# Local-attention scores from 64-row products in two PSUM banks, and a ring of two banks in place of three

## The reference, cut to what matters

```python
for i in range(DEPTH):                                    # 6
    x = attn_layer(shift_tokens(x), Wqkv[i], q_scale[i], k_scale[i], Wo[i]) + x
    x = ffn_layer(shift_tokens(x), ln_g[i], ln_b[i], W1[i], b1[i], W2[i], b2[i]) + x

def attn_layer(...):          # 16 heads of 64, windows of 32 tokens
    q = l2norm(q) * qs ; k = l2norm(k) * ksc              # then rotary tables on both
    sim = einsum('bhwie,bhwje->bhwij', bq, bk2) * 8.0     # bk2: keys of the window and of the one before
    attn = softmax(where(mask, -max, sim), -1)
    out = einsum('bhwij,bhwje->bhwie', attn, bv2)
    return out @ Wo
```

## Time and profile before

| What | Value |
|---|---|
| time, median of 3 runs | 1903.41 us (1899.98 to 1903.65) |
| span of the profiled execution | 1897.4 us |
| runs shown, lowest and highest, less that span | 2.6 and 6.3 us |
| TensorE clock granted, mean | 0.985 |
| PE busy | 1775.2 us (94%) |
| DVE busy | 1620.6 us (85%) |
| POOL busy | 1278.1 us (67%) |
| ACT busy | 1157.9 us (61%) |
| DMA queue q1 | 43.5% of 16 engines |

### The profile page before, as it was taken

The page is one execution under the profiler, slowest core; times in us unless marked ns, Lnnn a source line. Parts: engine busy times, 40 slices in busy tenths (PEclk is TensorE's granted clock), DMA queues, the critical chain, the costliest instruction groups (busy, mean ns, idle before and its releaser), DMA issues.

```text
span 1897.4 us, 49036 instructions
## 1 busy us (share of the span) xinstructions
PE 1775.2 (94%) x19119; PEld 1213.9 (64%) x19119; DVE 1620.6 (85%) x2695; ACT 1157.9 (61%) x2003; POOL 1278.1 (67%) x1548
## 2 busy tenths in 40 slices
PE   7999998899999999999999999999999999999997
PEld 4545454466666666666666676666666766666675
DVE  5887785799889999899898989998999889989983
ACT  3565665456566656665666666655766666666665
POOL 5212124777688777787777788768877778777762
PEclk8999999899999999999999999999999999999999
DMA  2000011455545555555455555555555455555552
GB/s 77 1 6 1 7 41 45 155 176 172 176 161 186 181 170 165 178 174 183 163 173 172 170 179 172 187 166 169 181 183 173 164 173 183 170 180 166 188 164 80
DMA packets 190739, 275.62 MB, mean 145 GB/s; under 512 B 23278, under 2 KB 87340, under 8 KB 190252
## 3 DMA queue, kind: packets, MB, share of 16 engines
q1 hardware_dynamic: 189004, 270.48, 43.5%
q10 hardware_dynamic: 1504, 2.00, 0.3%
HBM read 72.11 MB, written 52.43 MB: 66 GB/s over the span
## 4 chain that ended last, share of the span: by engine, by line
PE 37%; DVE 29%; POOL 14%; issue 10%; ACT 8%; DMA 1%; ACTq 0%; POOLq 0%; DVEq 0%; SPq 0%
DVE turned L982 10%; DVE kz L1002 7%; PE psum L597 4%; PE psum L668 3%; PE psum L599 3%; PE psum L598 3%; PE psum L807 3%; PE psum L837 3%; DVE rd L1018 3%; PE psum L691 3%; PE psum L682 3%; POOL u L1425 3%; PE psum L741 2%; POOL sdiff L1414 2%; ACT hid L1291 2%
## 5 line engine op out<-in xcount | busy, mean ns | idle before, releaser
L982 DVE SCALAR_TENSOR_TENSOR turned<-psum,vecs,tabs 128x1024 f32<-128x1024 f32 x384 | 486.8, 1268 | 33.2 <-POOL u L1425 20.9
L1190 ACT ACTIVATE sq<-psum 128x512 f32<-128x512 f32 x384 | 227.8, 593 | 164.8 <-PE psum L599 164.0
L1414 POOL TENSOR_TENSOR sdiff<-sdiff,rqs 128x512 f32<-128x512 f32 x192 | 200.8, 1046 | 151.9 <-DVE sdiff L1014 151.6
L1425 POOL TENSOR_TENSOR qT<-turned,swapped 128x512 f32<-128x512 f32 x192 | 242.4, 1283 | 37.9 <-PE psum L775 36.6
L1425 POOL TENSOR_TENSOR u<-turned,swapped 128x512 f32<-128x512 f32 x192 | 241.5, 1279 | 37.2 <-DMA swapped<-turned 36.8
L1002 DVE TENSOR_TENSOR kz<-u,psum 64x512 f32<-64x512 f32 x384 | 255.3, 665 | 6.3 <-PE psum L763 3.7
L796 PEld LDWEIGHTS psum<-pxT,v 128*64 128x64 f32 x6144 | 194.7, 138 | 74.3 <-issue 66.7
L1396 POOL TENSOR_TENSOR px<-px,rd 128x512 f32<-128x512 f32 x192 | 201.7, 1050 | 42.2 <-DVE rd L1020 39.7
L796 PE MATMUL psum<-pxT,v 128*64 128x64 f32 x6144 | 221.2, 225 | 4.3 <-DMA pxT<-scratch 4.2
L775 PE MATMUL psum<-kz,qT 128*32 128x128 f32 x6144 | 213.4, 277 | 6.0 <-DVE kz L1002 5.8
L597 PE MATMUL psum<-xs_hi,wqk_hi 128*128 128x512 f32 x384 | 176.4, 460 | 33.8 <-DVE turned L982 30.8
(11 more groups left out here) (187 smaller groups left out, 3475.7 us busy)
## 6 DMA issues: line engine op xcount, KB each, us to landing
swapped<-turned SPq DMA_DIRECT2D x384, 256.0 KB, 2.8
scratch<-pt SPq DMA_DIRECT2D x192, 256.0 KB, 2.1
pxT<-scratch SPq DMA_DIRECT2D x384, 128.0 KB, 2.8
v<-v SPq DMA_DIRECT2D x192, 192.0 KB, 2.5
w_raw<-in_wqkv SPq DMA_DIRECT2D x36, 256.0 KB, 3.3
v<-v SPq DMA_DIRECT2D x144, 64.0 KB, 2.0
wo<-in_wo SPq DMA_DIRECT2D x12, 256.0 KB, 3.4
w_raw<-in_w SPq DMA_DIRECT2D x12, 170.5 KB, 2.5
```

The source lines that it names most:

```text
L982: engine.scalar_tensor_tensor(out=turned[:, n % NROT, :, :], in0=both, scalar=vec(("ks" if which else "qs", i)), in1=tabs[:, 2 * which:2 * ...
L1190: engine.activation(sq[:, n % NSQ, :], bank(n % 2), ACT.Square).then_inc(s_sq, 1)
L1414: engine.tensor_tensor(sdiff[:, :, :], sdiff[:, :, :], r_, ALU.mult).then_inc(s_weigh, 1)
L1425: engine.tensor_tensor(u[:, n % GT, :] if which else qT[:, m_, :], turned[:, n % NROT, 0, :], swapped[:, n % NSWAP, :], ALU.add).then_inc( ...
```

## The change

The keys lose their zeros: `kT` has one copy of a pair's keys, on the same partitions as in `qT`. A score product takes 64 rows, one head's queries as weights and the same head's 64 key columns, so a unit has 32 products (64 records) where it had 16 (32 records). The first head of each pair writes bank 4 and the second writes bank 5. For each pair the four windows of the first head come first and then the four of the second. DVE writes the keys with one instruction of 128 partitions. The maxima, the differences and the mask go over both banks in one instruction each, with as many elements as before. The heads of a unit now lie as all first heads and then all second ones, so `apply` and the layout of `rqs` take other indices. The ring keeps banks 6 and 7, and a ring step waits for the one two places before. Eight clears of `kz` on POOL become one small one.

```diff
-        for m in range(HP):
-            put(0.02 * m - 0.1, "clear", m)
+        put(0.0, "clear")
...
-    kz = sb(ctx, "kz", [P, HP, 2, WIN + T])
+    kT = sb(ctx, "kT", [P, HP, WIN + T])
...
-    bank_b = ring("b", (5, 6, 7))
+    bank_b = ring("b", (6, 7))
+    score_banks = psum[:, 4:6, 0:MU * 2 * WIN]
...
-                    for w_ in range(4):
+                    for hp, w_ in itertools.product(range(2), range(4)):
                         t0 = (4 * t + w_) * WIN
-                        m = engine.matmul(bank(4)[WIN * w_:WIN * (w_ + 1), j * P:(j + 1) * P], qT[:, m_, t0:t0 + WIN],
-                                          kz[:, m_, :, t0:t0 + 2 * WIN], start=False, stop=j == MU - 1 and w_ == 3,
-                                          skip_group_check=True)
+                        rows = slice(DH * hp, DH * (hp + 1))
+                        m = engine.matmul(score_banks[WIN * w_:WIN * (w_ + 1), hp, j * 2 * WIN:(j + 1) * 2 * WIN],
+                                          qT[rows, m_, t0:t0 + WIN], kT[rows, m_, t0:t0 + 2 * WIN], start=False,
+                                          stop=j == MU - 1 and w_ == 3, skip_group_check=True)
...
-                                              (v1 if s_ else v0)[:, n % 2, 2 * j + hp, :], pxT[:, n % 2, s_, :, 2 * j + hp, :],
+                                              (v1 if s_ else v0)[:, n % 2, 2 * j + hp, :], pxT[:, n % 2, s_, :, MU * hp + j, :],
...
-                for hp in range(2):
-                    s_ = slice(64 * hp, 64 * hp + 64)
-                    m = engine.tensor_tensor(kz[s_, m_, hp, WIN:], u[s_, n % GT, :], nb[s_, :], ALU.mult)
-                m.then_inc(bank_n.empties(*step), 1)
+                engine.tensor_tensor(kT[:, m_, WIN:], u[:, n % GT, :], nb, ALU.mult).then_inc(bank_n.empties(*step), 1)
...
-                engine.tensor_reduce(smax[:, :], sv, AX_X, ALU.max).then_inc(s_smax, 1)
+                engine.tensor_reduce(smax[:, :].rearrange("p (h k) -> p h k", h=2), sv, AX_X, ALU.max).then_inc(s_smax, 1)
...
-                engine.tensor_tensor(sdiff[:, :, :], sv, mb, ALU.subtract).then_inc(s_sdiff, 1)
+                engine.tensor_tensor(sdiff[:, :, :].rearrange("p (h k) j -> p h k j", h=2), sv, mb, ALU.subtract).then_inc(s_sdiff, 1)
...
-                engine.copy(bank(4).rearrange("p (k j) -> p k j", j=2 * WIN), mask).then_inc(s_mask, 1)
+                engine.copy(score_banks.rearrange("p h (k j) -> p h k j", j=2 * WIN), mask).then_inc(s_mask, 1)
...
-                engine.memset(kz[:, m_, :, :], 0.0).then_inc(s_fill_d, 1)
+                engine.memset(kT[:, :, 0:WIN], 0.0).then_inc(s_fill_d, 1)
```

More of the change, by code:

```diff
@@ L730, in tensor @@
                 pe.wait_ge(*end_a)
-                engine.matmul(bank(4), selr[:, 0, :], selr[:, :, :].rearrange("k g p -> k (g p)"), start=True,
-                              stop=True).then_inc(s_blank, 1)
+                for j in (4, 5):
+                    m = engine.matmul(bank(j), selr[:, 0, :], selr[:, :, :].rearrange("k g p -> k (g p)"), start=True, stop=True)
+                m.then_inc(s_blank, 1)
             elif kind == "square_sums":
@@ L995, in vector @@
                 nb, r_ = bank_n.bank(*step), n // (2 * UT)
-                dve.wait_ge(s_fill_d, m_ + 1)
+                dve.wait_ge(s_fill_d, 1)
                 dve.wait_ge(s_rot, n + 1)
@@ L999, in vector @@
                 dve.wait_ge(*bank_n.full(*step))
-                for hp in range(2):
-                    s_ = slice(64 * hp, 64 * hp + 64)
-                    m = engine.tensor_tensor(kz[s_, m_, hp, WIN:], u[s_, n % GT, :], nb[s_, :], ALU.mult)
-                m.then_inc(bank_n.empties(*step), 1)
+                engine.tensor_tensor(kT[:, m_, WIN:], u[:, n % GT, :], nb, ALU.mult).then_inc(bank_n.empties(*step), 1)
             elif kind == "scores":
                 n, = k
-                sv = bank(4).rearrange("p (k j) -> p k j", j=2 * WIN)
-                mb = smax[:, :].rearrange("p (k o) -> p k o", o=1).broadcast_to([P, HU, 2 * WIN])
+                sv = score_banks.rearrange("p h (k j) -> p h k j", j=2 * WIN)
+                mb = smax[:, :].rearrange("p (h k o) -> p h k o", h=2, o=1).broadcast_to([P, 2, MU, 2 * WIN])
                 dve.wait_ge(s_scb, n + 1)
-                engine.tensor_reduce(smax[:, :], sv, AX_X, ALU.max).then_inc(s_smax, 1)
+                engine.tensor_reduce(smax[:, :].rearrange("p (h k) -> p h k", h=2), sv, AX_X, ALU.max).then_inc(s_smax, 1)
                 dve.wait_ge(s_smax, n + 1)
@@ L1213, in scalar @@
                 n, = k
-                mask = masks[:, 1 if n % TT == 0 else 0, :].rearrange("p (o j) -> p o j", o=1).broadcast_to([P, HU, 2 * WIN])
+                mask = masks[:, 1 if n % TT == 0 else 0, :].rearrange("p (h k j) -> p h k j", h=1, k=1).broadcast_to([P, 2, MU, 2 * WIN])
                 act.wait_ge(s_cb, 64)
@@ L1367, in gpsimd @@
             elif kind == "clear":
-                m_, = k
                 pool.wait_ge(*late_a)
-                engine.memset(kz[:, m_, :, :], 0.0).then_inc(s_fill_d, 1)
+                engine.memset(kT[:, :, 0:WIN], 0.0).then_inc(s_fill_d, 1)
             elif kind == "selr":
@@ L1447, in gpsimd @@
                 pool.wait_ge(s_weigh, TT * (g // 2 - NRQ + 1))
-                engine.tensor_tensor(rqs[:, g // 2 % NRQ, :, :].rearrange("p t (k r) -> p t k r", r=2), t_q, y_q,
+                engine.tensor_tensor(rqs[:, g // 2 % NRQ, :, :].rearrange("p t (h k) -> p t k h", h=2), t_q, y_q,
                                      ALU.mult).then_inc(s_qnorm, 1)
```

## The result

The changed kernel takes 1939.55 us (median, 1934.32 to 1943.81), and the kernel before took 1901.7 us in the same session. The ratio is 1.0194, 95% interval 1.017 to 1.0217. So it is slower by 38 us where the forecast was faster by 31 (1872 us, 67 under what was measured); the sign is wrong. The time lies inside the stated range of 1836 to 1945 only because the upper end of that range stood for a rival that did not happen.

What follows compares the result with a forecast made beforehand. PE and DVE, nearly equally loaded, were taken to bound the kernel. Per round -0.7, -2.5, +2.1, -0.5 and +0.3 made -1.3 us, -31 over 24 rounds: 1872 us, range 1836 to 1945.

Steps and rivals of the forecast that it cites:

- The keys: On DVE, 192 instructions of 691 ns replace 384: DVE loses 123 us; chain ceiling for the time 64 us.
- The three places of the ring: PE waits for copies at `token_major` 2.45 (elsewhere 1.97), second `up` 1.07, `down` 1.03 us; raw 110 us in all.
- The clears, the maxima, the mask: On POOL and over both score banks: counted at nothing; bounds for the clears 0 and -8 us.
- the walk round `token_major`: From `scores` (start s) to `apply`: s + 9.2 us against 9.9 before, 0.7 us shorter despite the late V copy.
- the size of a score step: On PE, eight groups of eight at 0.058 us: 0.46 us a step, 0.41 us less.
- what PE's saving is worth: The six score steps a round outside the `token_major` stretch count in full: 6 x -0.41 = -2.5 us.
- PE's wait for `turned`: Taken as 2.5 us a round, 1.0 inside the `token_major` stretch; 0.5 of the rest taken off.
- The 15.6 us for `xn`: PE waits behind POOL's statistics in some rounds, where products before save nothing; 0.3 us a round given back.
- the ring decides: Rival: late V copy costs its 2.45 us, waits exceed 3.8 us a round; +18 us, 1921 us; chance 0.16.
- the row halves in turn: Rival: score products on the two row halves run one after the other; +36 us, 1939 us; chance 0.14.
- the 27 ns feed: Rival: feeding limits score products to 27 ns a record, 1.74 us a step; +185 us, 2088 us; chance 0.10.
- forecast of 0.40 for slower: Chance of a slower kernel: ring decides 0.16, row halves in turn 0.14, feeding 0.10.

Runs made afterwards that it cites:

- keys_half: The kernel before, ring of three, without the DVE instruction that writes the second head's keys: 1868.37 us against 1902.78, ratio 0.9826.
- ring_two: The kernel before with only the ring cut to banks 6 and 7, bank 5 idle: 1977.83 us against 1902.78, ratio 1.0405.
- ring_two_keys_half: The kernel before with the ring of two and without DVE's instruction for the second head's keys: 1949.86 us, ratio 1.0249.

## Why the prediction was wrong

**What held.** The keys: 192 instructions at 647 ns in place of an estimated 691, and their effect on the time, -34 us alone, about half of the ceiling that I took from the chain. The three places of the ring and what they wait for: 2.2, 0.95 and 1.0 us now, against 2.45 (and 1.97), 1.07 and 1.03 read before. The clears, the maxima, the mask: nothing.

**The step that failed first: the walk round `token_major`.** I had s + 9.2 us from `scores` to `apply`, against 9.9 before, and so a gain of 0.7 in spite of the late copy. In the changed kernel it is 1090.50 to 1101.53, 11.0 us. In the kernel before it is 9.8 to 9.9 us in each of the 22 rounds from 400 to 1850 us; in the changed kernel it is 9.8 to 11.5, in the mean 10.8. DVE's and POOL's rows there show the cause:

```profile
1091.56 2.52 POOL L1423 TENSOR_TENSOR qT<-turned,swapped 128x512 f32<-128x512 f32 x2
1092.87 1.28 DVE L984 SCALAR_TENSOR_TENSOR turned<-psum,vecs,tabs 128x1024 f32<-128x1024 f32 x1 [0.74 <-POOL qT L1423]
1094.07 0.68 DVE L1008 TENSOR_REDUCE smax<-psum 128x8 f32<-128x512 f32 x1
1094.78 0.69 DVE L1013 TENSOR_TENSOR sdiff<-psum,smax 128x512 f32<-128x512 f32 x1
1095.55 1.04 POOL L1412 TENSOR_TENSOR sdiff<-sdiff,rqs 128x512 f32<-128x512 f32 x1 [0.47 <-DVE sdiff L1013]
```

I let DVE run ahead because it had lost work. But before the maxima it has `turned`, whose buffer POOL's `qT` must have read, and POOL's `qT` waits for the scores. DVE was some 0.7 us lighter and stood 0.74 us for POOL. It does so twice a round, 44 times in 22 rounds. DVE's waits for `qT` from 400 to 1850 us, in the kernel before, in keys_half, which has the ring of three and only DVE's work taken away, and in the changed kernel:

```profile
DVE turned L982 <- POOL qT L1425: 2.0, 4, 0.6
DVE turned L982 <- POOL qT L1425: 43.2, 45, 2.0
DVE turned L984 <- POOL qT L1423: 36.9, 44, 1.8
```

In ring_two, where DVE has all its work, it is 1.4 us in 3 places. So what DVE loses in work it stands for `qT`, and the chain scores, `qT`, `turned`, maxima, `weigh`, exponential, copy of V is one of dependences and not of load. `weigh` ended at 1096.59, 6.1 us after s, where I had 5.45; V's copy ended at 1098.33, s + 7.8, not 7.2. Behind the gap `scores` to `heads` took 0.92 us and `heads` to `apply` 1.58 us, where I had 0.60 and 0.89. This walk is 1.8 us off. About 0.8 of that is the clock (0.92 less the 0.79 of a step at the higher level, and 1.58 less 0.89), about 0.4 are the two score steps that came out too long (below), and about 0.5 is POOL's wait for DVE's differences. Over the 22 rounds it is 1.6 us off in the mean, 38 us over 24 rounds. It is 11.0 in the 16 rounds with the lower clock behind the gap and 10.2 in the six without, so that without any clock effect it would still be 1.0 over the forecast, and 0.3 over the kernel before.

**The second: the size of a score step.** The groups of four in the old trace gave 0.058 us for 64 columns, and I took the same for groups of eight. The step went from 1.01 to 0.79 us, not to 0.60: 0.22 saved in place of 0.41, some 36 us less on PE over the run. The direction was right (halves in turn are faster than halves apart), and the size off by half. What could not be read from a group of four is the pace of the records themselves, about 10 ns.

**The third: what PE's saving is worth.** I counted six of eight steps in full. With the ring of two the products gave 10 us net of the 42 that 192 x 0.22 make. A part of the rest went into the clock, which falls in twice as many places as in ring_two_keys_half. In rounds where it stays up, the walk takes 9.8 to 10.5 us in the changed kernel and 10.2 to 10.7 in ring_two_keys_half, so there most of the 0.44 of its two steps is won. That elsewhere a shorter step only makes the next wait for ACT or POOL longer is likely, and not shown.

**A term read from the wrong row.** I took the 57.1 us of the earlier trace rows for PE's wait for `turned`, 2.5 us a round. They are the weight loads' wait; PE's own was 23.4 us, 1.0 a round, and 0.80 of that lies in the walk itself. So some 0.2 were left outside it, and I took off 0.5: 7 us too much over 24 rounds. The 15.6 us for `xn` are the weight loads' too; PE's own were 10.3 us, in 5 places.

**The rival that came true** is "the ring decides", at 1921. It says that the late copy costs its full time and that waits of over 3.8 us a round decide. Measured are 85 us of ring waits over 22 rounds, 3.9 a round. Its price was too low since the product step gave only half, and the clock came on top. The rivals on the row halves in turn and on the 27 ns feed did not happen. That the first of these was priced at 1939 us, just what was measured, is chance: its step was to take 0.06 us more than before, and it took 0.22 less. The forecast of 0.40 for slower was too low for another reason: I saw 110 us of raw waits and let a walk through a single place cancel the largest.

**What stays open.** How much the clock costs is known to about 10 us and no better, and why it falls behind 16 of the 22 gaps and not behind the others is not known. What the products give at an equal clock is not measured. And the kernel with one copy of the keys, products into one bank and the ring of three is not built.

## What to carry to other kernels

A bank taken from a ring costs where an in-order engine copies late, and in this case these places could be read in the old trace: for each fill, when the copy of the step that would now be one nearer ended. Charge them in full unless every link of the chain that feeds the copy is seen to come earlier; an engine that has lost work still waits for the buffers that its neighbour frees. When waits like these appear, look first at the order of the copies. Moving two copies on ACT and one product on PE won back 43 us here, with a ring that cost 75, and each move was worth what the next wait behind it allowed.

## What the runs showed of the hardware

Products that go to the two row halves of the array, and to two banks, in turn take less time than with the halves kept apart: 0.79 us for 64 records against 0.93. These small records kept a pace of about 10 ns each, over 64 and over 128 of them, and no step measured was faster. A DVE product over 128 partitions took 647 ns, where one over 64 partitions had taken 665. PE gaps of 1.9 to 2.7 us at `token_major` were followed by 3.4 us at the lower clock level in 16 of 22 rounds. With idle products in the gap this happened in none, and that was worth 10 us, against an estimate of 29 from 17 stretches of 3.4 us at half speed.
